# Reordering the last draining slot of an eight-layer attention block ahead of its expert mixture

## The chip, the cores and the metric

The kernel runs on one core of one Trainium2 chip, as one program. The metric is the device time in microseconds of one execution. A core has five engines that run their own instruction streams in order and wait for each other by semaphores: TensorE (PE in the profile, with its weight loads as PEld), VectorE (DVE), ScalarE (ACT), GpSimd (POOL) and SyncE (SP), which only issues transfers here.

## The reference

The input is 8 sequences of 256 rows of 128 features, in float32. A conditioning vector gives a shift, a scale and a gate for two halves. The first half is eight layers of linear attention with a feed-forward of width 512; the second is a mixture of eight routed experts (the best two of each row) and a shared one.

```
h = layernorm(x) * (1 + ca) + sa
for each of 8 layers:
    q, k, v = h Wq + bq, h Wk + bk, h Wv + bv
    Q, K = elu(q) + 1, elu(k) + 1
    V = Q * sum(K * v) / (Q * sum(K) + eps)
    h = layernorm(gelu(V Wo + bo) + h) * ln1_s + ln1_b
    h = layernorm(gelu(gelu(h Wf1 + bf1) Wf2 + bf2) + h) * ln2_s + ln2_b      # FF1, FF2, the last norm
x = x + ga * h
h = layernorm(x) * (1 + cb) + sb
s = softmax(h router_w);  keep the two largest of 8
y = shared(h) + sum over experts of s_e * (silu(h gate_e) * (h up_e)) down_e
out = x + gb * y
```

## The kernel before, in words

The 2048 rows are cut into four chunks (`CH = 4`) of 512 rows; features lie on the 128 partitions. A piece of work (chunk c in layer l) has number n = 4 l + c, from 0 to 31 (`NI = 32`). The layers are software-pipelined in slots. Slot s holds four pieces at different stages: a = s (queries, keys, values), b = s - 1 (the output projection, the first norm), f = s - 2 (FF1 and FF2) and d = s - 3 (the last norm). Each engine has a function `slot` that writes its own share of a slot, and the order of its lines is the order on that engine; no scheduler moves anything. After the 32 full slots come two draining slots. In the first, `slot(NI, 0, ...)`, b, f and d are left. In the second, `slot(NI + 1, 1, ...)`, only f = 31 (chunk 3) and d = 30 (chunk 2) are left; this is the one that the change touches. Extra work is hooked into a slot by name: `run(extra, "place")` calls what the caller has given for that place.

Behind the draining slots comes the mixture. It runs in units: unit i of chunk c is `divmod(i, 10)`; units 0 and 1 of a chunk are halves of the shared expert, units 2 to 9 the routed experts. A unit is a gate product and an up product on TensorE, Silu on ScalarE, a product of the two on VectorE, and a down product on TensorE. Units 0 and 1 of the first chunk are plain float32 (`product`, L509), and a 128x512 float32 product is recorded as two matmuls. From unit 2 on every product is three matmuls of rounded operands (L511 to L513): the high part of weight and input (`wu_hi`, `h_hi`, written by ScalarE), and the low parts (`wu_lo`, `h_lo`, written by GpSimd in `split_weights_lo` L868 and `split_h` L883). `h_hi` and `h_lo` are the tiles xs_hi0, xs_lo0 and so on, so the profile shows them under those names. `ORDER` is the order in which the weights of the units are split. In the same way sg is the tiles ek and eq (the Silu of a unit), and su is mk and mq.

What the second draining slot does on each engine, and what waits for what:

- TensorE (L430 to L446): the last two quarters of FF1 (`ff1(1)`, `ff1(3)`, L404), then at the place "before ff2" the gate and up products of unit 0, then the first quarter of FF2 (L413), the transposes of the normalized piece 30 (xhD, L295, `to_fm["D"]`), the other three quarters of FF2. Behind the slot come the products of unit 1, then `weights_to_fm(0)` (L490), the transposes of the routing weights `cs`, then the gate of unit 2. `up(1)` writes the PSUM bank that FF2 used, so it waits for `g2_ready`. `weights_to_fm(0)` writes the bank that the gate of unit 0 used, so it waits for the first Silu (`sg_ready`). The gate of unit 2 waits for `h_hi`, `h_lo` and the first low part of the weights.
- ScalarE (L698 to L720): four Gelus of FF1, three splits `wu_hi`, the scale and shift of the last norm (`xs`, L712), then the Gelu of FF2 (L783), a table load, and the Silus of units 0 and 1 (L790), `scaled(1)` (zf) and the copy of the routing weights (cst, L759).
- GpSimd: the sum y2 = g2 + x2 of piece 30 (L844), the reciprocal root of the last norm's variance (rsD, L830, a power on 128x4), two weights' low parts, then the sum of piece 31 (L877), `split_h(0)`, two more low parts.
- VectorE: the first half of the routing (`route_scores`: mx, lg, cmp_gt, cmp_eq), the statistics of the last norm (stD, ..., veD, meanD), its normalization (xhD, L945), then `route_compare` (cmp_lo, cmp_all), ranks and weights (`cs`).

Of the kernel before, what the change touches and what calls it, by code (L numbers as in the profile page):

```python
# [30 lines left out]
def adaln_block(nc, x, w_qkv, w_o, w_f1, w_f2, v_a, v_bo, v_ln1, v_bf1, v_bf2, v_ln2, c_t, w_mod,  # L31
                w_router, w_unit, ident_in, select_in, lower_in, out):

    with ExitStack() as ctx:
# [145 lines left out]
        def has(n):  # L180

            return not isinstance(n, int) or 0 <= n < NI
# [107 lines left out]
        def _(pe):  # L290
# [32 lines left out]
            def slot(s, c, l, extra=None):  # L323
# [106 lines left out]
                if has(f):  # L430
                    ff1(1)
                    ff1(3)
                run(extra, "before ff2")
                if has(f):
                    ff2(0)
                run(extra, "middle")
                if has(b):
                    pe.wait_ge(y1_ready, b + 1)
                    transposes(ps_b, y1, to_tm["B"])
                if has(d):  # L440
                    pe.wait_ge(normed["D"], d + 1)
                    transposes(ps_d, xh["D"], to_fm["D"])
                if has(f):
                    ff2(1)
                    ff2(2)
                    ff2(3)  # L446

            slots(pe, slot, {"middle": rest_to_fm})


# [144 lines left out]
            keep_awake(9, ps_q)  # L595
            slot(NI + 1, 1, LAYERS, {"start": scores_0, "before ff2": unit_0})

# [31 lines left out]
        def _(act):  # L629
# [31 lines left out]
            act.wait_ge(consts_set, 4)  # L661

            def slot(s, c, l, extra=None):
                a, b, f, d = s, s - 1, s - 2, s - 3
# [28 lines left out]
                for j in range(FJ):  # L693
# [12 lines left out]
                    if j == 3 and has(a) and splits_next(s, c):  # L706
                        split_qkv_hi(l + 1)
                    if j == 3 and has(d):
                        act.wait_ge(to_fm["D"], d + 1)
                        if (c - 3) % CH == 0:  # L710
                            act.wait_ge(ld["vln2"], 4 * d + 16)
                        nc.scalar.activation(xs[(c - 3) % CH][:], ps_d[:], ACT.Identity,  # L712
                                             bias=vln2[:, 1:2], scale=vln2[:, 0:1]).then_inc(x_ready, 1)
                        if has(s + 1):
                            act.wait_ge(v_mm, d + 1)
                            nc.scalar.activation(xs_hi[(c - 3) % CH][:], ps_d[:], ACT.Identity,
                                                 bias=vln2[:, 1:2], scale=vln2[:, 0:1]).then_inc(x_hi_ready, 1)
# [66 lines left out]
            for i in range(CH * U):  # L784
# [3 lines left out]
                if i >= 2:  # L788
                    act.wait_ge(su_ready, i - 1)
                nc.scalar.activation(sg[i % 2][:], gates(i)[:], ACT.Silu).then_inc(sg_ready, 1)  # L790
                if splits(i) > splits(i - 1):

# [25 lines left out]
        def _(pool):  # L818
# [21 lines left out]
            def slot(s, c, l, extra=None):  # L840
                a, b, d = s, s - 1, s - 3
                if has(d):
                    pool.wait_ge(g2_ready, d + 1)
                    nc.gpsimd.tensor_tensor(y2[:], g2[:], x2[(c - 3) % CH][:], ALU.add).then_inc(y2_ready, 1)  # L844
                    rstd("D", d)
                if has(b):
# [23 lines left out]

            slots(pool, slot, None, None, {"last": lambda: split_x_lo(CH - 1, 0)})
            slot(NI, 0, LAYERS, {"end": lambda: rstd("F", 0)})
            split_weights_lo(ORDER[:2])
            slot(NI + 1, 1, LAYERS)
            split_weights_lo(ORDER[2:4])
            pool.wait_ge(g2_ready, NI)
            nc.gpsimd.tensor_tensor(y2[:], g2[:], x2[CH - 1][:], ALU.add).then_inc(y2_ready, 1)  # L877

            def split_h(c):
# [5 lines left out]

            split_h(0)
            split_weights_lo(ORDER[4:6])
            for i in range(FIRST, CH * U - 2):
# [20 lines left out]
        def _(dve):  # L909
# [230 lines left out]
            slot(NI, 0, LAYERS, {"within the last norm": select_rounded, "after the last norm": residual_0, "within the first norm": lambda: second_norm(0)})  # L1140
            slot(NI + 1, 1, LAYERS, {"before the last norm": lambda: route_scores(0)})
            route_compare(0)
            route_ranks(0)
# [93 lines left out]
```

## Time and profile before

| | us |
|---|---|
| median of 3 runs | 539.97 |
| lowest and highest | 539.44, 540.39 |
| the profiled execution | 542.1 |
| its span, first to last instruction | 540.3 |
| TensorE busy in the span | 507.2 (94%) |
| VectorE, ScalarE, GpSimd busy | 434.7, 407.7, 295.2 |
| mean granted TensorE clock | 0.989 of full speed |
| span of 400 to 420: TensorE busy | 19.85 |
| span of 420 to 440: TensorE busy | 16.90 |
| span of 440 to 460: TensorE busy | 15.92, at a clock of 0.91 |

The layers take the span up to about 410 us, the second draining slot lies at 409 to 420, the mixture behind it. Times are read as microseconds from the span's start. Busy time is that of the engine's records; TensorE's matmuls overlap by their tails, so the distance from one start to the next says what a matmul costs in a row of them, and not its recorded length. In brackets stand the idle time before an instruction and what ended it.

### The profile page before, as it was taken

How to read it: one execution, taken by the hardware profiler on the slowest of the kernel's cores; microseconds unless marked ns; L12 is line 12 of the kernel's file. 1: busy time of each engine (PE TensorE's matmuls, PEld its weight loads, DVE VectorE, ACT ScalarE, POOL GpSimd, SP SyncE). 2: the span in 40 equal slices, each digit the busy share in tenths (PEclk: the TensorE clock that was granted, in tenths of full speed). 3: DMA queues.
4: the chain of work that ended last, by engine and by line, in shares of the span. 5: the costliest groups of instructions: out<-in, count | busy, mean ns of one | idle time of the engine just before them, and what ended most of it. 6: DMA issues, size and time to landing. Idle time of an engine off the chain costs nothing.

```text
span 540.3 us, 8177 instructions
## 1 busy us (share of the span) xinstructions
PE 507.2 (94%) x1958; PEld 307.4 (57%) x1958; DVE 434.7 (80%) x1638; ACT 407.7 (75%) x594; POOL 295.2 (55%) x322
## 2 busy tenths in 40 slices
PE   2879999999999999999999999999999986999996
PEld 2335555565555556555555555555546565777784
DVE  4767988888888888889888888888887575977753
ACT  1748887888888888888888788888887555575752
POOL 3226556655565566555655665556545573555552
PEclk9979999999999999999999999999999998999999
DMA  7200000001000100100010010001000000000000
GB/s 245 82 0 16 6 21 20 15 5 39 15 5 5 34 15 5 39 15 0 5 39 15 5 36 18 0 5 39 0 2 0 1 1 2 0 19 2 20 13 28
DMA packets 15911, 11.22 MB, mean 21 GB/s; under 512 B 8189, under 2 KB 13693, under 8 KB 15893
## 3 DMA queue, kind: packets, MB, share of 16 engines
q1 hardware_dynamic: 15316, 10.42, 6.9%
q10 hardware_dynamic: 576, 0.60, 0.4%
q8 instruction: 7, 0.11, 0.1%
q14 instruction: 12, 0.09, 0.1%
HBM read 9.96 MB, written 1.05 MB: 20 GB/s over the span
## 4 chain that ended last, share of the span: by engine, by line
PE 80%; DVE 11%; issue 3%; POOL 2%; ACT 2%; DMA 1%; SPq 0%; ACTq 0%; DVEq 0%; POOLq 0%
PE bank L413 19%; PE bank L404 14%; PE bank L295 12%; PE bank L427 5%; PE bank L401 5%; PE bank L331 4%; PE bank L336 4%; PE bank L332 4%; PE bank L511 2%; PE bank L513 2%; PE bank L512 2%; PE bank L571 1%; DMA x<-in_x 1%; PE bank L556 1%; PE bank L559 1%
## 5 line engine op out<-in xcount | busy, mean ns | idle before, releaser
L413 PE MATMUL bank<-hid,wf 128*128 128x512 f32 x256 | 120.4, 593 | 0.0
L830 POOL TENSOR_TENSOR rsD<-veD,c_half 128x4 f32<-128x4 f32 x32 | 37.8, 1180 | 104.3 <-DVE veD L931 104.3
L404 PE MATMUL bank<-x,wf 128*128 128x512 f32 x192 | 93.0, 593 | 0.0
L698 ACT ACTIVATE hid<-bank,vbf 128x512 f32<-128x512 f32 x128 | 77.6, 693 | 0.3 <-PE bank L404 0.3
L902 POOL TENSOR_TENSOR xs_lo<-sc,xs_hi 128x512 fp32r<-128x512 f32 x36 | 47.8, 1327 | 46.9 <-ACT xs_hi L798 46.9
L413 PEld LDWEIGHTS bank<-hid,wf 128*128 128x128 f32 x256 | 46.0, 190 | 46.0 <-issue 30.6
L404 PEld LDWEIGHTS bank<-x,wf 128*128 128x128 f32 x192 | 35.1, 190 | 33.2 <-issue 16.2
L985 DVE TENSOR_SCALAR x<-bank,vln 128x256 f32<-128x256 f32 x64 | 31.9, 540 | 26.5 <-PE bank L295 26.5
L945 DVE TENSOR_SCALAR xhB<-bank,meanB,rsB 128x128 f32<-128x128 f32 x128 | 43.7, 405 | 7.8 <-POOL rsB L830 7.8
L945 DVE TENSOR_SCALAR xhD<-bank,meanD,rsD 128x128 f32<-128x128 f32 x128 | 43.7, 405 | 6.9 <-POOL rsD L830 2.7
L848 POOL TENSOR_TENSOR y<-g,xs 128x512 f32<-128x512 f32 x32 | 40.7, 1272 | 13.6 <-ACT g L692 13.5
L669 ACT ACTIVATE g<-bank,vbf 128x512 f32<-128x512 f32 x31 | 21.4, 690 | 34.7 <-PE bank L413 34.7
L295 PEld LDWEIGHTS bank<-ident,y 128*128 128x128 f32 x256 | 29.5, 140 | 31.4 <-POOL y L848 14.7
L331 PE MATMUL bank<-xs_hi,wqkv_hi 128*128 128x512 f32 x87 | 43.5, 500 | 1.4 <-DVE wqkv_lo L1057 0.6
L295 PE MATMUL bank<-ident,y 128*128 128x128 f32 x256 | 39.8, 278 | 4.4 <-ACT cst L759 2.3
L830 POOL TENSOR_TENSOR rsB<-veB,c_half 128x4 f32<-128x4 f32 x32 | 32.8, 1024 | 19.9 <-DVE veB L931 19.9
L672 ACT ACT_TABLE_LOAD x32 | 41.1, 1283 | 0.6
L692 ACT ACT_TABLE_LOAD x32 | 41.1, 1283 | 0.6
L844 POOL TENSOR_TENSOR y<-g,x 128x512 f32<-128x512 f32 x31 | 39.7, 1281 | 1.0 <-ACT g L669 1.0
L838 POOL TENSOR_TENSOR xs_lo<-xs,xs_hi 128x512 fp32r<-128x512 f32 x29 | 38.5, 1326 | 0.0
L427 PE MATMUL bank<-vt,wo 128*128 128x512 f32 x64 | 35.0, 628 | 1.1 <-DVE vt L1001 1.1
L336 PE MATMUL bank<-xs_lo,wqkv_hi 128*128 128x512 f32 x87 | 34.6, 452 | 0.0
(157 smaller groups left out, 1186.9 us busy)
## 6 DMA issues: line engine op xcount, KB each, us to landing
wf<-in_w_f SPq DMA_DIRECT2D x16, 256.0 KB, 2.6
wu<-in_w_unit SPq DMA_DIRECT2D x10, 192.0 KB
wqkv<-in_w_qkv SPq DMA_DIRECT2D x7, 192.0 KB, 2.4
x<-in_x SPq DMA_DIRECT2D x4, 256.0 KB, 6.7
out<-ot SPq DMA_DIRECT2D x4, 256.0 KB, 2.1
wo<-in_w_o SPq DMA_DIRECT2D x8, 64.0 KB, 1.8
wmod<-in_w_mod ACTq DMA_DIRECT2D x1, 384.0 KB, 4.0
vln<-in_v_ln SPq DMA_DIRECT2D x16, 1.0 KB, 1.7
```

The source lines that it names most:

```text
L295: mm = nc.tensor.transpose(out_bank[:, j * P:(j + 1) * P], t, ident[:])
L331: nc.tensor.matmul(bank[:], wqkv_hi[:, w], xs_hi[c][:], start=True, stop=False)
L336: return nc.tensor.matmul(bank[:], wqkv_hi[:, w], xs_lo[c][:], start=False, stop=True)
L404: mm = nc.tensor.matmul(ps_ff[j][:], wf1[:, j * P:(j + 1) * P], x2[(c - 2) % CH][:], start=True, stop=True)
L413: mm = nc.tensor.matmul(ps_f0[:], wf2[:, j, :], hid[:, j, :], start=(j == 0), stop=(j == FJ - 1))
L427: nc.tensor.matmul(ps_b[:], wo[:], vt[(c - 1) % CH][:], start=True, stop=True).then_inc(wo_mm, 1)
L672: nc.scalar.preload_act_table_set(LN_SET)
L692: nc.scalar.activation(g1[:], ps_b[:], ACT.Gelu_apprx_tanh, bias=vbo[:, 0:1]).then_inc(g1_ready, 1)
L698: nc.scalar.activation(hid[:, j, :], ps_ff[j][:], ACT.Gelu_apprx_tanh, bias=vbf1[:, j:j + 1]).then_inc(h_ready, 1)
L830: nc.gpsimd.tensor_tensor(rs[buf(k, n)][:], ve[buf(k, n)][:], c_half[:], ALU.pow).then_inc(rstd_ready[k], 1)
L902: nc.gpsimd.tensor_tensor(sc_lo[k % 2][:], sc[i % 3][:], sc_hi[k % 2][:].bitcast(F32), ALU.subtract).then_inc(sc_lo_ready, 1)
L945: ap = nc.vector.tensor_scalar(rows_of(k, n)[:, j, :], src[:, j, :], mean[q][:, j:j + 1], rs[q][:, j:j + 1], ALU.subtract, ALU.mult)
```

## The change

On TensorE, in the slot without a piece b, the four quarters of FF2 come directly behind FF1, then the transposes of the last norm, then unit 0 and unit 1. On ScalarE the last norm's scale is written behind the first Silu. On GpSimd `split_h(0)` and the low part of the third weight in `ORDER` go between the sum y2 and rsD, three low parts follow rsD, and the sum of piece 31 comes last. On VectorE `route_compare(0)` goes ahead of the last norm's normalization. No instruction is added or removed, and the slots of the layers are written as before.

```diff
-                run(extra, "before ff2")
                 if has(f):
                     ff2(0)
                 run(extra, "middle")
...
-                if has(d):
+
+                def last_norm_to_fm():
                     pe.wait_ge(normed["D"], d + 1)
                     transposes(ps_d, xh["D"], to_fm["D"])
+
+                if has(d) and has(b):
+                    last_norm_to_fm()
                 if has(f):
                     ff2(1)
                     ff2(2)
                     ff2(3)
+                if has(d) and not has(b):
+                    last_norm_to_fm()
+                run(extra, "behind ff2")
...
-            slot(NI + 1, 1, LAYERS, {"start": scores_0, "before ff2": unit_0})
+            slot(NI + 1, 1, LAYERS, {"start": scores_0, "behind ff2": unit_0})
...
-                    if j == 3 and has(d):
+                    if j == 3 and has(d) and has(b):
+                        last_norm(c, d)
...
                 nc.scalar.activation(sg[i % 2][:], gates(i)[:], ACT.Silu).then_inc(sg_ready, 1)
+                if i == 0:
+                    last_norm(1, NI - 2)
...
                     nc.gpsimd.tensor_tensor(y2[:], g2[:], x2[(c - 3) % CH][:], ALU.add).then_inc(y2_ready, 1)
+                    run(extra, "behind the sum")
                     rstd("D", d)
...
+            def first_low_parts():
+                split_h(0)
+                split_weights_lo(ORDER[2:3])
+
             slot(NI, 0, LAYERS, {"end": lambda: rstd("F", 0)})
             split_weights_lo(ORDER[:2])
-            slot(NI + 1, 1, LAYERS)
-            split_weights_lo(ORDER[2:4])
+            slot(NI + 1, 1, LAYERS, {"behind the sum": first_low_parts})
+            split_weights_lo(ORDER[3:6])
             pool.wait_ge(g2_ready, NI)
             nc.gpsimd.tensor_tensor(y2[:], g2[:], x2[CH - 1][:], ALU.add).then_inc(y2_ready, 1)
-            split_h(0)
-            split_weights_lo(ORDER[4:6])
...
-            slot(NI + 1, 1, LAYERS, {"before the last norm": lambda: route_scores(0)})
-            route_compare(0)
+            slot(NI + 1, 1, LAYERS, {"before the last norm": lambda: route_scores(0),
+                                     "within the last norm": lambda: route_compare(0)})
             route_ranks(0)
```

TensorE before, from the second half of FF1 in the second draining slot to the gate of unit 2 (x2_3 is the input of FF1, hid that of FF2, hf0 that of the mixture; bank2 takes the gate of unit 0 and then the routing weights, bank3 the sum of FF2 and then the up product of unit 1):

```order
L404 MATMUL bank4<-x2_3,wf1 128x512
L404 MATMUL bank0<-x2_3,wf1 128x512
L509 MATMUL bank2<-hf0,wu 128x512
L509 MATMUL bank5<-hf0,wu 128x512
L413 MATMUL bank3<-hid,wf2 128x512
L295 MATMUL bank6<-ident,xhD 128x128 x4
L413 MATMUL bank3<-hid,wf2 128x512 x3
L509 MATMUL bank4<-hf0,wu 128x512
L509 MATMUL bank3<-hf0,wu 128x512
L490 MATMUL bank2<-ident,cs 16x128 x4
L511 MATMUL bank0<-xs_hi0,wu_hi 128x512
```

And TensorE now, at the same place:

```order
L404 MATMUL bank4<-x2_3,wf1 128x512
L404 MATMUL bank0<-x2_3,wf1 128x512
L413 MATMUL bank3<-hid,wf2 128x512 x4
L295 MATMUL bank6<-ident,xhD 128x128 x4
L515 MATMUL bank2<-hf0,wu 128x512
L515 MATMUL bank5<-hf0,wu 128x512
L515 MATMUL bank4<-hf0,wu 128x512
L515 MATMUL bank3<-hf0,wu 128x512
L496 MATMUL bank2<-ident,cs 16x128 x4
L517 MATMUL bank0<-xs_hi0,wu_hi 128x512
```

Unit 0 (banks 2 and 5) has moved behind FF2 and the transposes, so that eight recorded matmuls of units 0 and 1 now stand between FF2 and the routing weights, where four stood.

GpSimd before, from the sum of piece 30 to the first low part of a unit's product (xs_lo0 from hf0 is `h_lo`):

```order
L844 TENSOR_TENSOR y2<-g2,x2_2 128x512
L830 TENSOR_TENSOR rsD<-veD,c_half 128x4
L868 TENSOR_TENSOR wu_lo<-wu,wu_hi 128x384 x2
L877 TENSOR_TENSOR y2<-g2,x2_3 128x512
L883 TENSOR_TENSOR xs_lo0<-hf0,xs_hi0 128x512
L868 TENSOR_TENSOR wu_lo<-wu,wu_hi 128x384 x2
L902 TENSOR_TENSOR xs_lo2<-sc2,xs_hi2 128x512
```

And GpSimd now:

```order
L855 TENSOR_TENSOR y2<-g2,x2_2 128x512
L888 TENSOR_TENSOR xs_lo0<-hf0,xs_hi0 128x512
L880 TENSOR_TENSOR wu_lo<-wu,wu_hi 128x384
L841 TENSOR_TENSOR rsD<-veD,c_half 128x4
L880 TENSOR_TENSOR wu_lo<-wu,wu_hi 128x384 x3
L900 TENSOR_TENSOR y2<-g2,x2_3 128x512
L915 TENSOR_TENSOR xs_lo2<-sc2,xs_hi2 128x512
```

`h_lo` and one weight have moved ahead of rsD, and the sum that waits for the Gelu of FF2 has moved to the end.

## Rows read from the trace of the kernel before

**Rows 1.** The page, part 4: the chain that ended last, by engine.

```profile
PE 80%; DVE 11%; issue 3%; POOL 2%; ACT 2%; DMA 1%; SPq 0%; ACTq 0%; DVEq 0%; POOLq 0%
```

**Rows 2.** Timeline of PE, 412 to 424: start, length, instruction, idle before.

```profile
413.82 1.88 PE L509 MATMUL bank<-hf,wu 128*128 128x512 f32 x4
415.54 1.02 PE L413 MATMUL bank<-hid,wf 128*128 128x512 f32 x2
416.56 0.66 PE L295 MATMUL bank<-ident,xhD 128*128 128x128 f32 x4
417.06 2.74 PE L413 MATMUL bank<-hid,wf 128*128 128x512 f32 x6
419.63 2.07 PE L509 MATMUL bank<-hf,wu 128*128 128x512 f32 x4
422.57 0.60 PE L490 MATMUL bank<-ident,cs 128*16 128x128 f32 x4 [0.88 <-ACT ek L790]
423.44 0.47 PE L511 MATMUL bank<-xs_hi,wu_hi 128*128 128x512 f32 x1 [0.27 <-issue]
```

**Rows 3.** Timeline of ACT, 412 to 425.

```profile
413.17 1.84 ACT L698 ACTIVATE hid<-bank,vbf 128x512 f32<-128x512 f32 x3 [0.29 <-PE bank L404]
...
417.26 0.78 ACT L712 ACTIVATE xs<-bank,vln 128x512 f32<-128x512 f32 x1 [1.01 <-PE bank L295]
419.83 0.69 ACT L783 ACTIVATE g<-bank,vbf 128x512 f32<-128x512 f32 x1 [1.80 <-PE bank L413]
...
421.83 0.60 ACT L790 ACTIVATE ek<-bank 128x512 f32<-128x512 f32 x1
...
424.42 0.60 ACT L790 ACTIVATE ek<-bank 128x512 f32<-128x512 f32 x1 [0.25 <-PE bank L513]
```

**Rows 4.** Timeline of POOL, 404 to 450.

```profile
408.89 1.27 POOL L844 TENSOR_TENSOR y<-g,x 128x512 f32<-128x512 f32 x1
414.01 1.02 POOL L830 TENSOR_TENSOR rsD<-veD,c_half 128x4 f32<-128x4 f32 x1 [3.86 <-DVE veD L931]
415.00 1.96 POOL L868 TENSOR_TENSOR wu_lo<-wu,wu_hi 128x384 fp32r<-128x384 f32 x2
...
421.82 1.27 POOL L883 TENSOR_TENSOR xs_lo<-hf,xs_hi 128x512 fp32r<-128x512 f32 x1
```

**Rows 5.** Timeline of DVE, 404 to 460, around the last norm of piece 30.

```profile
410.57 0.42 DVE L1097 TENSOR_TENSOR cmp_gt<-lg 128x256 f32<-128x256 f32 x1
...
412.37 0.89 DVE L914 BATCH_NORM_STATS2 stD<-bank 128x6 f32<-128x128 f32 x4 [1.03 <-PE bank L295]
...
415.14 1.37 DVE L945 TENSOR_SCALAR xhD<-bank,meanD,rsD 128x128 f32<-128x128 f32 x4 [1.13 <-POOL rsD L830]
...
419.15 0.19 DVE L1122 TENSOR_TENSOR cs<-comb,cs 128x32 fp32r<-128x32 f32 x1
```

**Rows 6.** Timeline of all engines, 443 to 447, rows of DVE and POOL.

```profile
443.27 1.30 POOL L883 TENSOR_TENSOR xs_lo<-hf,xs_hi 128x512 fp32r<-128x512 f32 x1
...
443.63 1.23 DVE L1097 TENSOR_TENSOR cmp_gt<-lg 128x256 f32<-128x256 f32 x1
...
444.52 1.50 POOL L902 TENSOR_TENSOR xs_lo<-sc,xs_hi 128x512 fp32r<-128x512 f32 x1
...
444.77 1.52 DVE L1098 TENSOR_TENSOR cmp_eq<-lg 128x256 f32<-128x256 f32 x1
```

**Rows 7.** Timeline of all engines, 243.5 to 245.5, one slot of the layers.

```profile
243.87 1.18 POOL L830 TENSOR_TENSOR rsD<-veD,c_half 128x4 f32<-128x4 f32 x1 [3.43 <-DVE veD L931]
...
244.59 0.42 DVE L1024 TENSOR_SCALAR mq<-eq 128x512 f32<-128x512 f32 x1
```

**Rows 8.** Timeline of PE, 430 to 460.

```profile
448.73 0.50 PE L571 MATMUL bank<-cst,sel 128*128 128x512 f32 x1 [1.81 <-DVE sc L1177]
...
457.68 0.63 PE L295 MATMUL bank<-ident,y 128*128 128x128 f32 x4 [2.28 <-ACT cst L759]
```

**Rows 9.** Windows: length, busy of PE, PEld, DVE, ACT, POOL, then PEclk.

```profile
449.00:453.00 4.00, 4.00 (x12) 3.13 (x12) 2.99 (x9) 1.56 (x3) 2.58 (x2) 0.57 0.01 2
```

More of the change, by code:

```diff
@@ L661, in _, with last_norm @@
             act.wait_ge(consts_set, 4)
+            def last_norm(c, d):
+                act.wait_ge(to_fm["D"], d + 1)
+                if (c - 3) % CH == 0:
+                    act.wait_ge(ld["vln2"], 4 * d + 16)
+                nc.scalar.activation(xs[(c - 3) % CH][:], ps_d[:], ACT.Identity,
+                                     bias=vln2[:, 1:2], scale=vln2[:, 0:1]).then_inc(x_ready, 1)
             def slot(s, c, l, extra=None):
@@ L707, in slot @@
                         split_qkv_hi(l + 1)
-                    if j == 3 and has(d):
[L709 to L713, printed above, removed]
+                    if j == 3 and has(d) and has(b):
+                        last_norm(c, d)
                         if has(s + 1):
@@ L871, in _ @@
             slots(pool, slot, None, None, {"last": lambda: split_x_lo(CH - 1, 0)})
-            slot(NI, 0, LAYERS, {"end": lambda: rstd("F", 0)})
-            split_weights_lo(ORDER[:2])
-            slot(NI + 1, 1, LAYERS)
-            split_weights_lo(ORDER[2:4])
-            pool.wait_ge(g2_ready, NI)
-            nc.gpsimd.tensor_tensor(y2[:], g2[:], x2[CH - 1][:], ALU.add).then_inc(y2_ready, 1)
             def split_h(c):
@@ L884, in split_h @@
                                         ALU.subtract).then_inc(h_lo_ready, 1)
-            split_h(0)
-            split_weights_lo(ORDER[4:6])
+            def first_low_parts():
+                split_h(0)
+                split_weights_lo(ORDER[2:3])
+            slot(NI, 0, LAYERS, {"end": lambda: rstd("F", 0)})
+            split_weights_lo(ORDER[:2])
+            slot(NI + 1, 1, LAYERS, {"behind the sum": first_low_parts})
+            split_weights_lo(ORDER[3:6])
+            pool.wait_ge(g2_ready, NI)
+            nc.gpsimd.tensor_tensor(y2[:], g2[:], x2[CH - 1][:], ALU.add).then_inc(y2_ready, 1)
             for i in range(FIRST, CH * U - 2):
```

## The prediction

> **What bounds the kernel now.** I read the page first. Its chain that ended last is 80% TensorE [rows 1], so only a change of what TensorE waits for can move the end. I then took TensorE's timeline through the stretch that the diff touches, the second draining slot and the start of the mixture, and last the timelines of ScalarE, GpSimd and VectorE there, to see who releases each wait.
>
> The reader is to see in [rows 2] that TensorE is dense up to the end of unit 1 and then stops twice. Matmuls of 128x512 in float32 start 0.43 us apart (four from 413.82 to 415.54). The two of FF2's first quarter should give way at 416.40, and the transposes of xhD start at 416.56, when VectorE has ended xhD at 415.14 + 1.37 = 416.51 [rows 5]. The four transposes take 0.50 from their start to the next row's. The last four matmuls of the draining part (unit 1) take 2.07 and not 1.88: `up(1)` waits for the Gelu of FF2, which ends at 419.83 + 0.69 = 420.52 [rows 3]. Then L490 starts at 422.57 on the first Silu (421.83 to 422.43), though unit 1 had ended its starts at 419.63 + 1.72 + 0.19 = 421.54: 1.03 lost, of which the profile calls 0.88 idle. Last, the gate of unit 2 starts at 423.44. From L490's start to that it is 0.87. Four transposes took 0.50 above with the change to the next kind of row in it; these write 16 rows in place of 128, and I take 0.40 for them, so 0.47 are lost, of which 0.27 is marked idle. That is put down to "issue", but GpSimd ends `h_lo` at 421.82 + 1.27 = 423.09 [rows 4], so that is the wait.
>
> **The change part by part.** It adds and removes nothing, so the sum is the idle time that goes. From 413.82 to 423.44 TensorE has to do: FF2, eight matmuls at 0.43 = 3.44; four transposes 0.50; units 0 and 1, eight matmuls = 3.44; L490, 0.40. That is 7.78 in 9.62 us, 1.84 less. The four losses above (0.16, 0.19, 1.03, 0.47) make 1.85, the same within rounding. It comes in full if nothing is late in the new order. I take the waits one by one.
>
> FF2 starts at 413.82 in place of 415.54. Its quarters need the four hidden Gelus; three of them run from 413.17 and end at 415.01 [rows 3], and the last quarter is reached at 413.82 + 2.58 = 416.40. Nothing waits. FF2 ends its starts at 417.26.
>
> The transposes of xhD are then reached at 417.26, where xhD was ready at 416.51, so there is 0.75 of room. Two edits eat into it. GpSimd now does `h_lo` (1.27) and one weight (0.98, half of the 1.96 for two in rows 4) between the sum, which ends at 410.16, and rsD, which starts at 414.01: both are over before rsD can start, so rsD itself is not held. `h_hi`, which `h_lo` needs, is written by ScalarE before that sum ends. But they now lie beside cmp_gt and cmp_eq on VectorE, and [rows 6] show what that does: cmp_gt takes 1.23 and not the 0.42 of [rows 5], and ends 0.29 behind the end of GpSimd's subtraction (444.57); cmp_eq again takes 1.52 and ends 0.27 behind the next (446.02), which itself takes 1.50 and not 1.30. Laid on the new order: `h_lo` ends at 411.43, cmp_gt at 411.72, the weight's low part at 411.43 + 0.98 + 0.20 = 412.61, cmp_eq at 412.88. The statistics stD started at 412.37, when the transposes of y2 were done; now they start at about 412.92, 0.55 late. This carries to rsD (414.56) and to the start of the normalization (415.69). The other edit, cmp_lo and cmp_all ahead of the normalization, costs 2 x 0.42 and two gaps of 0.05, 0.94, and fits in the 1.13 for which VectorE waits for rsD [rows 5]. xhD is then ready at 417.06 + 0.05. TensorE comes at 417.26: still not late. If the port costs nothing, the room is 0.75; if cmp_lo and cmp_all are held too, it turns into a stall (first rival). So the price of these two edits is 0 to 1.25, and I take 0, the end that the nearest row speaks for: [rows 7] show VectorE's mq, 0.42 for 128x512, fully inside a power of GpSimd on 128x4 (243.87 to 245.05): the power does not hold VectorE off.
>
> The Trainium skill, page "SBUF — State Buffer", section "SBUF: two separate sides", says that the shared port pair is an exclusive lock for the whole instruction and that the other engine fully blocks, for a VectorE operation in a two-port mode or with two SBUF inputs. Rows 6 agree. Rows 7 do not where GpSimd's instruction is the power; what the rule would make of this change is the first rival.
>
> Unit 0 follows at 417.26 + 0.50 = 417.76, unit 1 at 419.48, and L490 is reached at 421.20. `up(1)` starts at 420.34 and needs the Gelu of FF2. That Gelu started 0.19 behind the last start-to-start of FF2 (417.06 + 2.58 = 419.64, to 419.83), so now 417.45, and ends at 418.14: the 0.19 are gone. ScalarE is free for it, since the scale of the last norm no longer stands ahead. The first Silu came 2.00 behind the Gelu's start (421.83 - 419.83, the table load in it), so now at 419.45, and ends at 420.05: 1.15 before L490 asks for it. The scale (0.78, rows 3) goes behind it and pushes the second Silu to about 420.6, when its gate (419.48 + 0.86 = 420.34) is done. It also pushes what follows. From the first Silu to that of unit 2 it was 424.42 - 421.83 = 2.59, 0.25 of it idle; with the scale in it, 2.34 + 0.78 = 3.12, so ScalarE is free for the Silu of unit 2 at 422.57. TensorE will have its gate done at 424.42 - 1.84 = 422.58. This is a tie; a tenth late would be hidden, since TensorE still has the up products of unit 2, a down product and a broadcast ahead of what needs it. That broadcast needs the moved scale (ended by 420.9) and the routing weights' copy, which precedes the Silu of unit 2, and stands two microseconds behind the gate.
>
> The routing weights `cs` were done at 419.34, 2.83 behind the end of xhD [rows 5], with cmp_lo and cmp_all in it (0.94 at least). So seven small operations take 1.9 at most, and now start at 417.1 behind xhD. But three low parts and the sum of piece 31 (from about 415.6 to 419.8 on GpSimd) lie beside them. With none held, `cs` comes at 419.0; with three of them held by 0.8 each, as cmp_gt was, at 421.4, 0.2 behind the moment when L490 is reached. So 0 to 0.2, taken as 0.
>
> Every low part is earlier than it was: `h_lo` at 411.4, the first three weights by 412.6, the next three by about 418.8. The sum of piece 31 ends by 419.9 and is first read at 457.68 [rows 8]. So the gate of unit 2 starts at 421.20 + 0.40 = 421.60 against 423.44. Behind it every engine waits for what TensorE started there, and no transfer is in play, so the mixture moves as one piece.
>
> Sum: -1.84 + 0 + 0 = -1.84. The profiled execution took 542.1 (span 540.3, 1.8 around it) and would take 540.3. The median of the runs is 539.97, 2.1 below the profiled one; the stretch is short and has no transfers in it, so I take the same difference from the median: 538.1.
>
> **The rivals.**
>
> *The port held for every instruction.* If the power did hold VectorE off, cmp_lo (issued at 414.6) would wait for the end of rsD at 415.58 and end at 415.87; the next low part would end at 415.6 + 1.2 = 416.8 and cmp_all at 417.1; xhD at 418.5. TensorE stands from 417.26 to 418.5, 1.25. `cs` is then done about 420 to 422, at the time when L490 comes. Net -0.6: 539.4. For it: rows 6. Against: rows 7. The page of the Trainium skill named above, taken at its word, would give this time.
>
> *The clock, once more.* Right behind an idle time of 1.81 [rows 8] TensorE's granted clock falls: from 449 to 453 it is 0.57 of full speed [rows 9], which means that for most of this stretch it stood at the lower of its two levels, 1.2 GHz. Against full speed that costs 4.00 x (1 - 0.57) = 1.72. Behind the longer idle time of 2.28 [rows 8] the profile shows no such stretch. So length alone does not decide, and a mixture that runs 1.8 earlier may meet it elsewhere. One stretch more: -1.84 + 1.72 = -0.1, 539.9. One less: -3.6, 536.4.
>
> *Slower: the clock, twice more.* The same mechanism, with its place in the mixture's idle times (before 448.73, before 457.68, and later ones). It decides from 1.84 us of added half-speed time, more than one stretch: two cost 3.44, net +1.6, 541.6. For it: the mixture keeps its idle times, and one was followed by the lower level. Against: the longer one was not, and the change takes idle time away ahead of them.
>
> *It does not do what it says.* If the wait for `h_lo` or the first Silu only changed hands, for instance if the Silu is held by the table load, L490 would move less. That load began when the Gelu had ended, since the Silu came 1.31 behind it, and nothing else stands before it, so I see no place for this and fold its chance into the first rival.
>
> **How the numbers follow.** Forecast 0.72; the port 0.09, 539.4; one more half-speed stretch 0.07, 539.9; one less 0.06, 536.4; two more 0.06, 541.6. What a measurement can tell from no change is 0.2%, 1.08 us: below 538.9 is faster, above 541.0 slower. Faster: 0.72 + 0.06 = 0.78. Same: 0.09 + 0.07 = 0.16. Slower: 0.06. The forecast's own range is 537.6 to 538.7 (the price of the port from 0 to 0.7, and the scatter of the runs shown). The range runs from the case of one less, 536.4, to a little over the port's, 539.6; it leaves out the two higher cases, 0.13 together.
>
> **What would show it.** In the profile after: FF2's eight matmuls at once behind FF1, xhD's transposes without idle time in front, units 0 and 1 in one row of eight, L496 (the former L490) directly behind with no wait for ScalarE, and the gate of unit 2 at about 421.6. cmp_gt and cmp_eq of the first chunk longer together by some 1.5 us. The first Silu at about 419.5 and the scale behind it. The prediction is wrong if the transposes of xhD wait for VectorE by more than 0.3, if L496 waits for `cs`, or if the distance from the gate of unit 2 to the end of the span (540.3 - 423.4 = 116.9) is not what it was within a few tenths; a longer one with a clock of 0.50 in a further window is the clock's doing.

## The result and the profile after

| | before | changed |
|---|---|---|
| median, us | 539.82 (13 runs) | 535.88 (13 runs) |
| lowest, highest | 537.56, 541.40 | 534.94, 538.27 |
| the profiled execution, its span | 542.1, 540.3 | 535.88, 533.7 |
| mean granted TensorE clock in it | 0.989 | 1.00 |

The ratio is 0.9928, with a 95% interval of 0.9909 to 0.9947: faster by 3.9 us, twice the 1.84 that were forecast, and outside the range. (One later run of the kernel before, of 737.73 us, was in a slow state and is left out of everything below.) The draining slot did what was forecast. TensorE's timeline of the changed kernel, 408 to 419 (columns as in [rows 2]):

```profile
409.00 1.88 PE L404 MATMUL bank<-x,wf 128*128 128x512 f32 x4
410.72 3.60 PE L413 MATMUL bank<-hid,wf 128*128 128x512 f32 x8
414.15 0.64 PE L295 MATMUL bank<-ident,xhD 128*128 128x128 f32 x4
414.62 3.60 PE L515 MATMUL bank<-hf,wu 128*128 128x512 f32 x8
418.06 0.60 PE L496 MATMUL bank<-ident,cs 128*16 128x128 f32 x4
418.42 0.48 PE L517 MATMUL bank<-xs_hi,wu_hi 128*128 128x512 f32 x1
```

No row has idle time. From the second half of FF1 (L404 x4) to the gate of unit 2 it is 418.42 - 409.00 = 9.42. Before it was 423.44 [rows 2] - 412.10 = 11.34, from this row of the kernel before:

```profile
412.10 1.88 PE L404 MATMUL bank<-x,wf 128*128 128x512 f32 x4
```

So 1.92 are won (forecast 1.84). I call this distance the draining distance below. The other engines there, first VectorE:

```profile
407.47 1.09 DVE L1110 TENSOR_TENSOR cmp_gt<-lg 128x256 f32<-128x256 f32 x1
408.48 1.22 DVE L1111 TENSOR_TENSOR cmp_eq<-lg 128x256 f32<-128x256 f32 x1
409.73 0.89 DVE L927 BATCH_NORM_STATS2 stD<-bank 128x6 f32<-128x128 f32 x4
...
411.28 0.42 DVE L1115 TENSOR_TENSOR cmp_lo<-cmp_eq,lower 128x256 f32<-128x256 f32 x1
411.73 0.43 DVE L1116 TENSOR_TENSOR cmp_all<-cmp_gt,cmp_lo 128x256 f32<-128x256 f32 x1
412.71 1.37 DVE L958 TENSOR_SCALAR xhD<-bank,meanD,rsD 128x128 f32<-128x128 f32 x4 [0.55 <-POOL rsD L841]
```

then GpSimd:

```profile
407.01 1.26 POOL L888 TENSOR_TENSOR xs_lo<-hf,xs_hi 128x512 fp32r<-128x512 f32 x1
408.23 1.18 POOL L880 TENSOR_TENSOR wu_lo<-wu,wu_hi 128x384 fp32r<-128x384 f32 x1
411.37 1.21 POOL L841 TENSOR_TENSOR rsD<-veD,c_half 128x4 f32<-128x4 f32 x1 [1.95 <-DVE veD L944]
```

and ScalarE:

```profile
414.35 0.69 ACT L792 ACTIVATE g<-bank,vbf 128x512 f32<-128x512 f32 x1 [1.21 <-PE bank L413]
...
416.35 0.60 ACT L799 ACTIVATE ek<-bank 128x512 f32<-128x512 f32 x1
416.85 0.77 ACT L673 ACTIVATE xs<-bank,vln 128x512 f32<-128x512 f32 x1
```

cmp_gt and cmp_eq are held by GpSimd (2.31 together, against twice the 0.42 of [rows 5]). cmp_lo starts 0.09 before the power rsD, and cmp_all lies wholly inside it (411.73 to 412.16, the power from 411.37 to 412.58); they take their usual 0.42 and 0.43, and the power 1.21 in place of the 1.02 of [rows 4]. xhD ends at 414.08, and TensorE comes for it at 410.72 + 3.44 = 414.16: 0.08 in hand. The first Silu ends at 416.95, 1.11 before the L496 that waits for it. The routing weights `cs` are written at 417.17, 0.89 before it.

Where are the other 4.7 us of the 6.6 by which the two profiled spans differ? Windows of the kernel before (columns as in [rows 9]):

```profile
25.00:40.00 15.00, 10.52 (x25) 4.75 (x26) 9.83 (x39) 7.47 (x9) 3.34 (x5) 0.77 0.00 0
445.00:455.00 10.00, 8.19 (x31) 6.17 (x30) 7.49 (x16) 5.71 (x9) 3.79 (x4) 0.83 0.00 1
```

and of the changed kernel, the second moved with the mixture:

```profile
25.00:40.00 15.00, 10.47 (x35) 5.11 (x34) 9.61 (x37) 9.50 (x14) 5.70 (x9) 1.00 0.00 0
440.00:450.00 10.00, 7.02 (x32) 4.97 (x30) 7.48 (x16) 6.82 (x13) 4.87 (x4) 1.00 0.00 1
```

The reader is to see the PEclk of 0.77 and 0.83 against 1.00: the kernel before has stretches in which TensorE runs at half of its full clock, which I call half-speed stretches, and this profile of the changed kernel has none in these windows. The L404 row already starts 3.1 earlier (409.00 against 412.10), from the start of the program, which the change doesn't touch. From the gate of unit 2 to the end of the span it is 533.7 - 418.42 = 115.28 against 116.86: 1.58 less, with the same instructions. So 6.6 = 3.1 + 1.9 + 1.6, and only the middle term is the new order's own. The question of the experiments was whether the rest is luck of the two profiled executions or belongs to the change.

### The profile page after: what moved, and what is told of

It is laid out like the page before. It is cut to its first block, busy times and chain, and to the rows that moved or that the text cites. A ratio compares the mean times of both kernels' runs of the same rounds, so it can differ in the third digit from the quotient of the medians.

```text
span 533.7 us, 8177 instructions
## 1 busy us (share of the span) xinstructions
PE 501.3 (94%) x1958; PEld 304.6 (57%) x1958; DVE 437.0 (82%) x1638; ACT 407.7 (76%) x594; POOL 295.7 (55%) x322
## 3 DMA queue, kind: packets, MB, share of 16 engines
HBM read 9.96 MB, written 1.05 MB: 21 GB/s over the span
## 4 chain that ended last, share of the span: by engine, by line
PE 81%; DVE 11%; issue 3%; POOL 2%; ACT 2%; DMA 1%; SPq 0%; ACTq 0%; DVEq 0%; POOLq 0%
PE bank L413 19%; PE bank L404 14%; PE bank L295 12%; PE bank L427 5%; PE bank L401 5%; PE bank L331 4%; PE bank L336 4%; PE bank L332 4%; PE bank L519 2%; PE bank L517 2%; PE bank L518 2%; PE bank L577 1%; PE bank L562 1%; DMA x<-in_x 1%; DVE sc L1190 1%
## 5 line engine op out<-in xcount | busy, mean ns | idle before, releaser
L404 PE MATMUL bank<-x,wf 128*128 128x512 f32 x192 | 93.0, 593 | 0.0
L404 PEld LDWEIGHTS bank<-x,wf 128*128 128x128 f32 x192 | 35.0, 189 | 33.3 <-issue 16.3
L860 POOL TENSOR_TENSOR y<-g,xs 128x512 f32<-128x512 f32 x32 | 40.8, 1275 | 11.5 <-ACT g L705 11.3
```

The lines of the kernel that those rows point to most:

```text
L404: mm = nc.tensor.matmul(ps_ff[j][:], wf1[:, j * P:(j + 1) * P], x2[(c - 2) % CH][:], start=True, stop=True)
```

## The experiments

The runs fall into four groups (e1 to e4, e5 to e8, e9 to e12, e13 to e16), each with its own runs of the kernel before beside it; their medians were 540.22, 540.78, 539.80 and 540.58, their mean clocks 0.9910, 0.9889, 0.9904 and 0.9895. The ratios are taken within a group; medians and clocks of different groups compare less well. "Clock" is the mean over a kernel's runs of the granted clock; "draining" and "to the end" are the draining distance and the distance from the gate of unit 2 to the end of the span, in its profile.

| kernel | median us | ratio [95%] | clock | draining | to the end |
|---|---|---|---|---|---|
| before, repeated (e1) | 541.00 | 1.0001 [0.9982, 1.0020] | 0.9898 | 11.34 | 116.80 |
| changed, repeated (e2) | 537.08 | 0.9942 [0.9920, 0.9964] | 0.9928 | 9.43 | 115.35 |
| TensorE's order alone (e3) | 537.98 | 0.9977 [0.9952, 1.0003] | 0.9911 | 10.07 | 116.88 |
| the rest alone (e4) | 540.10 | 1.0005 [0.9986, 1.0024] | 0.9906 | 11.51 | 116.85 |
| before, mixture filled (e5) | 538.49 | 0.9963 [0.9937, 0.9989] | 0.9938 | 11.34 | 115.29 |
| changed, mixture filled (e6) | 537.16 | 0.9935 [0.9912, 0.9958] | 0.9930 | 9.43 | 115.27 |
| changed, moved back 17 (e7) | 539.26 | 0.9983 [0.9962, 1.0005] | 0.9900 | 11.27 | 116.79 |
| before, drain filled (e8) | 541.73 | 1.0012 [0.9982, 1.0042] | 0.9883 | 11.35 | 117.39 |
| before, pushed 18 (e9) | 540.94 | 1.0036 [1.0009, 1.0063] | 0.9900 | 12.78 | 115.23 |
| changed, GpSimd as before (e10) | 537.17 | 0.9946 [0.9925, 0.9968] | 0.9935 | 9.38 | 115.29 |
| before, start filled (e11) | 538.13 | 0.9962 [0.9945, 0.9979] | 0.9968 | 11.34 | 116.80 |
| changed, start filled (e12) | 536.38 | 0.9944 [0.9922, 0.9965] | 0.9972 | 9.43 | 115.28 |
| before, both filled (e13) | 537.25 | 0.9938 [0.9918, 0.9958] | 0.9996 | 11.34 | 115.22 |
| changed, both filled (e14) | 534.93 | 0.9894 [0.9867, 0.9921] | 0.9990 | 9.41 | 115.24 |
| changed, moved back 5 (e15) | 538.84 | 0.9967 [0.9946, 0.9989] | 0.9917 | 9.96 | 115.93 |
| changed, moved back 11 (e16) | 539.53 | 0.9980 [0.9955, 1.0005] | 0.9900 | 10.61 | 115.25 |

**The two kernels again.** e1 is the kernel before and e2 the changed one, without an edit.

> The kernel before, word for word, as a second program: what the comparison gives for no change, and a second profile of it. Theory A (the 1.84 us of the draining slot are shifted in full, and the rest of the measured 3.9 is TensorE's clock, which falls to its lower level by chance of the execution): ratio 1.000 within 0.3%; the distance from the second half of FF1 in the second draining slot (L404 x4) to the gate of unit 2 is 11.3 us again; the profile's half-speed stretches (span 28 to 37 and 449 to 453 before) lie elsewhere or are absent, and the runs' spans go down as their clock goes up. Theory B (the stretch at 449 to 453 belongs to the order of the kernel before, by the idle time in its draining slot): it is there again, between the broadcast that waits for sc and the routing weights' transposes of chunk 1.

> The changed kernel again, with a second profile. Both theories: ratio 0.990 to 0.996 to the kernel before; the distance from the second half of FF1 (L404 x4) to the gate of unit 2 is 9.4 us again, 1.9 less. Theory A: with the clock at full in both, the spans differ by 1.9; some of these runs have a half-speed stretch in the mixture too. Theory B: no run of this kernel has one in the mixture.

Both draining distances repeat to 0.01. e1 has the half-speed stretch behind the same broadcast, e2 has none there. Theory A had called that chance. Against the runs beside it e2 gains 3.1 us (0.9942), less than the 3.9 of the first comparison, though inside its interval. Over all groups the kernel before gave 130 runs with a recorded clock and the changed one 19 (13 of them from the first comparison), which can be laid side by side by their clock:

| clock of the run | before: runs, mean us | changed: runs, mean us |
|---|---|---|
| under 0.9875 | 34, 541.8 | 0 |
| 0.9875 to 0.9905 | 42, 540.7 | 3, 538.1 |
| 0.9905 to 0.9935 | 40, 539.4 | 2, 537.6 |
| 0.9935 to 0.9965 | 6, 538.4 | 8, 536.0 |
| over 0.9965 | 8, 538.3 | 6, 535.7 |

In a row the kernels differ by 1.8 to 2.6. The rest is that the changed kernel's runs stand in lower rows of the table. 3 and 2 runs in two of the rows are few. That the changed kernel has the better clock rests most on the first comparison: its 13 runs have a mean of 0.9954, e2's six have 0.9928, only 0.0018 above the kernel before beside them, and e10's twelve (the changed kernel but for GpSimd, below) 0.9935, 0.0031 above.

**The parts.** e3 takes TensorE's half of the diff, e4 everything else.

```diff
# e3, on the kernel before; e4 is the changed kernel with the same lines turned back
-                run(extra, "before ff2")
...
+                if has(d) and not has(b):
+                    last_norm_to_fm()
+                run(extra, "behind ff2")
```

> Only TensorE's order is changed (FF2, last norm's transposes, then units 0 and 1); ScalarE, GpSimd and VectorE are as in the kernel before. From the rows of before: the scale of the last norm stands ahead of the Gelu of FF2 again and waits for the transposes (reached at 417.26 in the time of before, so it runs 417.9 to 418.6), so the Gelu ends at 419.3, the first Silu at 421.2 (L490 asks at 421.2), the sum of piece 31 at 420.6 and h_lo at 421.8; gate of unit 2 at 422.1 against 421.6 in the full change and 423.4 before. So the distance from FF1's second half to it is 10.0 (before 11.3, full change 9.4). If instead the other engines' moves are what counts: 11.3. Ratio 0.996 to 0.998 with equal clocks.

> Only ScalarE, GpSimd and VectorE are changed, TensorE's order is that of before. h_lo is early, so the 0.47 before the gate of unit 2 go; cmp_gt and cmp_eq are held by GpSimd (together 2.3 and not 0.84), so xhD comes 0.3 to 0.55 later, and here TensorE asks for it at 416.40 with no room, so FF2 and with it the Gelu and the first Silu are late by that. Distance from FF1's second half to the gate of unit 2: 11.2 to 11.5, no gain. If low parts were the bound in the draining slot: 10.9 or less.

Both distances came as expected: 10.07 (10.0) and 11.51 (11.2 to 11.5). In e3 ScalarE's timeline shows why 0.65 are missing:

```profile
414.35 0.78 ACT L718 ACTIVATE xs<-bank,vln 128x512 f32<-128x512 f32 x1 [1.65 <-PE bank L295]
415.02 0.68 ACT L789 ACTIVATE g<-bank,vbf 128x512 f32<-128x512 f32 x1
```

The Gelu of FF2 stands behind the scale, and `h_lo` behind the sum behind the Gelu. In e4, xhD is late by the port and TensorE waits for it (timeline of PE):

```profile
414.07 0.65 PE L295 MATMUL bank<-ident,xhD 128*128 128x128 f32 x4 [0.68 <-DVE xhD L952]
```

**GpSimd's move by itself.** e10 is the changed kernel with `split_h(0)` and the low parts where they were.

```diff
-            slot(NI + 1, 1, LAYERS, {"behind the sum": first_low_parts})
-            split_weights_lo(ORDER[3:6])
+            slot(NI + 1, 1, LAYERS)
+            split_weights_lo(ORDER[2:4])
             (the sum of piece 31)
+            split_h(0)
+            split_weights_lo(ORDER[4:6])
```

> The changed kernel with GpSimd's order of before (h_lo behind the sum of piece 31). In e3 the gate of unit 2 came 0.65 later than in the full change; there the Gelu of FF2 stood behind the scale of the last norm. With ScalarE's move kept, the Gelu ends at 415.04 (times of the changed kernel's profile), the sum at 416.35, h_lo at 417.6, and the gate is reached at 418.42: distance from FF1's second half 9.4, the same as the full change. cmp_gt and cmp_eq take 0.42 each again. If GpSimd's move carries a gain of its own, the distance is 9.9 (0.47 more). Time within 0.2% of the changed kernel by either, if the clock is the same.

9.38: the move of the low parts is worth nothing once the Gelu comes early. e10 keeps ScalarE's and VectorE's moves, which e3 lacks; of the two it is ScalarE's one instruction that e3's timeline points at. No run moved it alone.

**Filling the mixture's idle time.** Transposes of the identity into banks that nobody reads at that time:

```diff
+                    if u == 6 and n == 1: pe.wait_ge(x_new, 2);    keep_awake(14, ps_q)   # ahead of norm_to_fm
+                if i == 9:                pe.wait_ge(hf_ready, 2); keep_awake(16, ps_v)   # ahead of the broadcast
+                if i == U + 2:            pe.wait_ge(lg_ready, 2); keep_awake(18, ps_q)   # ahead of last_to_tm
```

> The kernel before, with transposes of the identity into free PSUM banks placed on TensorE where the mixture of the first two chunks waits: 14 ahead of the transposes of xhF, 16 ahead of the broadcast that waits 1.81 for sc, 18 ahead of the transposes that wait 2.28 for cst. They start about 0.11 us apart, so they fill 1.5, 1.8 and 2.0 us of idle time and delay nothing by more than 0.1. Both theories: the half-speed stretch that the profiles of the kernel before, of its repeat and of both half changes have behind that broadcast (3.3 to 3.4 us, worth 1.7) is gone, the mean clock of the runs goes up from 0.991 by 0.003 to 0.994, the median down by 1 to 1.7: ratio 0.997 to 0.998. If filling does not hold the clock: ratio 1.000 to 1.001.

> The changed kernel with the same fillers. Theory A2 (the change raised the clock only by where its idle times fall, and it is still at risk of a half-speed stretch in the mixture): median 0.3 to 1 us lower than the changed kernel. Both: with fillers in both, the two kernels differ by the draining slot alone, 1.9 (e5 to e6: 0.9965). If the change had its extra 2 us from anywhere but the clock, e5 and e6 would still be 3.5 to 4 apart.

e5's window (8.19 and 0.83 in the kernel before):

```profile
445.00:455.00 10.00, 9.94 (x56) 8.09 (x55) 8.29 (x17) 6.80 (x11) 5.37 (x5) 1.00 0.01 2
```

The fillers hold the clock, and the kernel before gains 0.37% by them (2.0 us) without any change of its own work. The changed kernel gains nothing (537.16 against 537.08 and 535.88): it had no stretch there to lose in its profiles. The medians of e5 and e6 are 1.3 apart, their means 1.7, where the kernels themselves were 3.9 apart. With the mixture's waits filled in both, nothing is left beyond the 1.92 of the draining slot, within the scatter of 12 runs each.

**Position or idle time?** e7 gives the gain back as dense work ahead of the mixture, e8 takes the draining slot's idle time away and leaves the mixture where it was. In these cuts and the next two the `wait_ge` ahead of the transposes is left out.

```diff
 # e7, on the changed kernel, behind weights_to_fm(0)     # e8, on before
+  if i == 2: keep_awake(17, ps_q)                        +  if i == 1: keep_awake(8, ps_q)   # ahead of weights_to_fm(0)
                                                          +  if i == 2: keep_awake(3, ps_q)
```

> The changed kernel, with 17 transposes of the identity between the routing weights' transposes and the gate of unit 2: the 1.9 us won in the draining slot are given back as dense work of TensorE, with no idle time, so the mixture stands where it stood before. Theory P (the half-speed stretch depends on where the mixture's idle times fall in time, counted from the start of the program): it is back in the profile behind the broadcast that waits for sc, mean clock 0.991, ratio 0.999 to 1.001. Theory I (it depends on the idle time in the draining slot, which is gone here too): no such stretch, mean clock 0.995, ratio 0.996 to 0.997.

> The kernel before, with 8 transposes ahead of the routing weights' transposes and 3 ahead of the gate of unit 2, into idle time only: the draining slot has no idle time to speak of and the mixture starts within 0.1 of where it did. Theory P: nothing changes, stretch in the profile, mean clock 0.991, ratio 0.999 to 1.001. Theory I: no stretch, mean clock 0.995, ratio 0.996 to 0.997.

e7's mean clock is 0.9900, where e2 has 0.9928 and the first runs of the changed kernel 0.9954. Its ratio alone would not show that: the 1.84 us put back are 0.0034, and 0.9942 + 0.0034 = 0.9976 lies inside e7's interval. Its windows have the PEclk of the kernel before to the digit:

```profile
25.00:40.00 15.00, 10.88 (x27) 5.24 (x28) 8.71 (x32) 7.40 (x10) 4.30 (x6) 0.77 0.00 0
445.00:455.00 10.00, 6.75 (x24) 4.96 (x23) 5.77 (x14) 5.30 (x11) 3.88 (x3) 0.83 0.00 1
```

and e8, with no idle time in its draining slot, has two stretches in the mixture:

```profile
445.00:455.00 10.00, 7.95 (x29) 5.73 (x27) 6.86 (x16) 5.20 (x9) 3.81 (x4) 0.83 0.00 1
455.00:465.00 10.00, 8.00 (x32) 6.58 (x33) 5.87 (x18) 4.09 (x9) 3.76 (x4) 0.83 0.01 2
```

So theory I is out: e8 has no better clock than the kernel before beside it (0.9883 against 0.9889), and e7 has the stretch without idle time in the draining slot. Theory P is left, that what counts is when the mixture's idle times come. Three more positions:

```diff
+  if i == 2: keep_awake(18, ps_q)      # e9, on before;  5 and 11 on the changed kernel: e15, e16
```

> The kernel before, with 18 transposes of the identity between the routing weights' transposes and the gate of unit 2. The gate starts 1.5 us later, with dense work ahead of it. Theory P (where the mixture's idle times fall, counted from the start of the program, decides on the half-speed stretch): 1.9 us earlier lost it, and 1.5 us later may lose it too; then the mean clock goes from 0.990 to 0.993 or more and the added 1.5 cost little: ratio 0.998 to 1.001. Theory N (the stretch has nothing to do with the position, e7 and e8 showed it by chance): clock 0.990, ratio 1.003.

> The changed kernel with 5 transposes (0.55 us) ahead of the gate of unit 2, so the mixture starts 0.5 later, dense. If the position decides smoothly, between none (mean clock 0.994) and 17 (0.990): 0.993, and 0.5 to 0.9 us over the changed kernel. If there is an edge in it, 0.994 and +0.5, or 0.990 and +1.9.

> The same with 11 transposes (1.2 us). Smooth: clock 0.9915, 2.0 us over the changed kernel. If position plays no part and e7 was chance: clock 0.994, +1.2.

On the changed kernel the mean clock is lower with more transposes, 0, 5, 11 and 17: 0.9946 (19 runs), 0.9917, 0.9900, 0.9900. But these stand in different groups. Against the kernel before in the same group it is +0.0018 (e2), +0.0023, +0.0005 and +0.0011, each known to 0.002 or 0.003 only, so the steps between them are not shown. By the ratios e15 stands 1.4 us above e2 and 2.1 above the first comparison, 0.5 of it its own dense work, and the intervals overlap. e9, on the far side, is a partial miss: its profile has no stretch in the mixture, and 3 of its 12 runs have a clock of 0.995 or more, but 5 have 0.984. Theory P had hoped for more; the ratio is what theory N said. The runs of one kernel scatter over both cases; that position shifts the shares is likely and not proved.

The profiles tell more than theory P. Counted from the start of the span, position does not decide: the gate of unit 2 starts at 420.45 in both e2 and e4, and only e4 has the stretch. Counted from the end of the start's own stretch it fits, in the three profiles where that end is the same, 36.01 in e1 and e15 and 36.02 in e2. Windows of e1, then of e15, with the mixture's waits from their timelines of PE:

```profile
29.18:36.01 6.83, 5.79 (x10) 2.06 (x8) 3.70 (x18) 2.60 (x4) 1.27 (x2) 0.50 0.00 0
36.01:449.01 413.00, 404.48 (x1540) 233.40 (x1539) 352.03 (x1406) 341.97 (x484) 239.07 (x264) 1.00 0.06 14
449.01:452.43 3.42, 3.42 (x10) 2.64 (x9) 2.68 (x8) 1.23 (x2) 2.38 (x2) 0.50 0.01 2
...
448.37 0.50 PE L571 MATMUL bank<-cst,sel 128*128 128x512 f32 x1 [1.81 <-DVE sc L1177]
```

```profile
29.18:36.01 6.83, 5.74 (x10) 2.06 (x8) 3.67 (x18) 2.64 (x4) 1.23 (x2) 0.50 0.00 0
36.01:455.85 419.84, 410.15 (x1572) 238.44 (x1572) 359.01 (x1417) 346.56 (x494) 243.11 (x267) 1.00 0.05 14
455.85:459.26 3.41, 3.41 (x12) 2.73 (x10) 2.03 (x8) 1.09 (x2) 2.24 (x2) 0.50 0.03 5
...
447.05 0.50 PE L577 MATMUL bank<-cst,sel 128*128 128x512 f32 x1 [1.81 <-DVE sc L1193]
454.46 0.63 PE L295 MATMUL bank<-ident,y 128*128 128x128 f32 x4 [2.28 <-ACT cst L771]
```

The same wait of 1.81 is followed by the lower clock in e1, where it ends at 448.37, and not in e15, where it ends 1.32 earlier; there the wait of 2.28 is. In e2 it ends at 445.73 and neither is. In before, e1, e7 and e8 the clock falls 413.0 behind the end of the start's stretch (before: 449.42 - 36.41), but 0.17 to 1.03 behind the end of the wait; in e4, the fifth profile with both, whose stretch at the start is half as long, it falls 416.4 behind. So the time of the fall goes with the start's stretch, and not with the end of the wait.

**The start.** Slots 1 and 2 filled in the same way (e11, e12), and both places filled (e13, e14).

```diff
+  slot 1: keep_awake(6, ps_y) ahead of v, 8 ahead of the output projection, 18 ahead of the transposes of y1
+  slot 2: keep_awake(14, ps_y) ahead of v
```

> The kernel before, with fillers in slots 1 and 2 (6, 8 and 18 transposes in slot 1, 14 in slot 2, into the bank of the modulation) where TensorE waits 0.7 to 2.1 us between 20 and 31 us of the span. Half-speed stretches between 25 and 40, which come in most profiles, of 3 to 12 us, should go: mean clock 0.996, runs closer together, median 1.5 to 2.5 us lower (ratio 0.996); the stretch behind the broadcast in the mixture stays, as theory P has it while the mixture moves no further than the spread of the runs. If the fillers do not hold the clock at the start, ratio 1.000 to 1.002.

> The changed kernel with the same fillers at the start. With the start at full clock in both, e11 and e12 differ by the draining slot (1.9) and by the mixture's half-speed stretch (1.7, if e11 has it and e12 has not): 3.6. If the stretch comes in both or in none, 1.9. This should be the fastest kernel so far: 533.5 to 535, ratio 0.988 to 0.991.

> The kernel before with the fillers of e5 (mixture) and of e11 (start) together. No half-speed stretch at either place: mean clock 0.998 or more in most runs, 536.5 to 537.5, ratio 0.993 to 0.995.

> The changed kernel with both sets of fillers. With the clock at full in both, e13 and e14 differ by the draining slot alone: 1.9 (1.6 to 2.2). If they differ by 3 or more, the extra of the measured 3.9 is not the clock. 534.5 to 535.5, ratio 0.989 to 0.992, the fastest median of all kernels.

The start's stretches go. e11 still has one in the mixture in its profile and e12 has none, but over the runs their clocks are equal (0.9968, 0.9972), and they differ by 1.75, not by the 3.6 that I expected. Three of e12's six runs have a clock of 0.995 to 0.996, as the profiles with one stretch in the mixture alone have (0.995 in e11, 0.996 in e3), so the changed kernel probably meets the stretch in some of its executions too. With the start at full clock the changed kernel has no better clock than the kernel before. e13 and e14, at 0.9996 and 0.9990, differ by 2.3 in median and in mean (1.9 expected, 1.6 to 2.2 allowed for, so 0.1 over that, and well under the 3 that would have spoken against the clock); in their profiles the draining distances differ by 1.93 and the ways to the end by 0.02. e14's windows:

```profile
25.00:40.00 15.00, 13.74 (x65) 8.27 (x63) 10.49 (x39) 9.46 (x13) 4.70 (x7) 1.00 0.01 1
440.00:455.00 15.00, 14.62 (x86) 12.03 (x85) 10.59 (x27) 9.82 (x17) 6.20 (x6) 1.00 0.01 2
```

It is the fastest median of all, 534.93, 1.1% under the kernel before, with 5 runs.

## Why the prediction was wrong

**The order on TensorE: right.** 1.92 against 1.84, with FF2, transposes and units in one dense row. The price of the port was right too: the statistics start 0.73 behind the second half of FF1 and not 0.27, 0.46 late (0.55 forecast), xhD 0.08 ahead of TensorE (0.15 forecast), the power no hindrance to cmp_lo and cmp_all, as [rows 7] had it. The Silu came 7.35 behind the second half of FF1, as worked out (419.45 - 412.10). `cs` came 8.17 behind it, between the two cases worked out (6.9 and 9.3). By the Trainium skill, page "SBUF — State Buffer", section "SBUF: two separate sides", cmp_all with its two SBUF inputs should have waited for the power, which had started before it; it took 0.43 inside it, so the measurement decides against the rule for this GpSimd instruction, and for it with the subtractions.

**GpSimd's move: its own gain was counted in a loss that two edits remove.** The 0.47 of wait for `h_lo` go by the early Gelu alone (e10). The sum was not harmed.

**The step that failed** is "the stretch is short and has no transfers in it, so I take the same difference from the median", with the chance of 0.06 given to one half-speed stretch less. It takes the clock's losses outside the draining slot as the same before and after. They were not, and the prediction's own sign of being wrong came: from the gate of unit 2 to the end it is 115.28 and not 116.9. The stretch behind the broadcast was in the profiles of the kernel before, e1, e4, e7, e8 and e11, all with the mixture at its old place behind FF1, and in that of e3, 1.3 earlier; it was in none of the changed kernel, e2, e10 and e12, 1.9 earlier. The other positions do not make a smooth row: e9 (1.4 later), e15 (1.4 earlier) and e16 (0.7 earlier) lack it too. Without a stretch the mixture takes 115.2 to 115.4, with this one 116.8 to 116.9, so it costs 1.55 (1.72 forecast). Behind the later wait of 2.28, where e8 and e15 have one, it costs only 0.6 to 0.7 (117.39 against 116.8, 115.93 against 115.25). 1.92 + 1.55 = 3.5 of the 3.9. The case was among the rivals, at 536.4, and its size was nearly right; its chance was argued from two idle times of one profile, as if a single execution showed what the runs do.

**How much of it is luck.** The first comparison is the most favourable of three. e2 gains 3.1 us and e10, with the same draining distance, 2.9. The forecast's ratio, 538.1 / 539.97 = 0.9965, lies just above e2's interval and inside e10's. So the clock's share is 2.0 us in the first comparison and 1.0 to 1.2 in the two others.

**What stays open.** Why the position counts. It seems to count only while the start has its own half-speed stretches (e7 against e11 and e12), and the fall stands 413.0 behind their end in four of five profiles. Whether these stretches set the times of the later falls, or only show times that are set by something else, no run tested. The Trainium skill, page "TensorE: Matmul & The Clock Gate", section "Part 1: The HAM clock gate (the "warmup" mystery)", says that the gate's window is free-running and does not start anew with a kernel. If programs also started evenly over it, and nothing at the start shifted the rest, all positions would be equal over many runs. e7, none of whose 12 runs has a clock over 0.993 where 14 of the changed kernel's 19 do, speaks against the three taken together; which of them fails is not shown. Also open are 0.4 us, between the 2.3 of e13 and e14 and the 1.92 of the trace, within the scatter of 9 and 5 runs.

## What to carry to other kernels

Before a difference of profiled spans is explained, split it at two or three instructions that both traces have: here 6.6 fell into 3.1 of start, 1.9 of the change and 1.6 of clock. Where an idle time of TensorE is followed by a stretch at its lower clock, an edit ahead of it that moves it in time can put that stretch at stake, for good or ill, and a forecast needs the clocks of several runs and not of one. The same holds for the measurement: three comparisons of the reordering (the last without GpSimd's move) gave 3.9, 3.1 and 2.9 us. Filling such waits with transposes of the identity into a free bank cost nothing that could be measured here (the draining distances of e8 and e13 are those of the kernel before, to 0.01); at both places it took 3.3 us off the kernel before (540.58 to 537.25), and it makes two kernels comparable.

## What the runs showed of the hardware

- A wait of 1.81 us on TensorE was followed by half-speed clock in one execution (e1) and not in another (e15) whose half-speed stretch at the start was alike to 0.01 us and where the wait ended 1.32 us earlier. In four profiles (before, e1, e7, e8) of the five that have both, the fall came 413.0 us behind the end of the start's half-speed stretch, in the fifth (e4) 416.4.
- A half-speed stretch of 3.4 us cost 1.55 us behind the wait for the broadcast and 0.6 to 0.7 us behind the wait of 2.28 us.
- A power on 128x4 on GpSimd and a two-input VectorE instruction on SBUF run beside each other: 1.21 in place of 1.02 for the one, 0.43 for the other (cmp_all), where its usual time is 0.42. A subtraction on GpSimd, of 128x512 or 128x384, holds the same kind of instruction: cmp_gt and cmp_eq took 1.09 and 1.22 in place of 0.42 and ended 0.29 behind it. In e10, without the subtractions beside them, they took 0.42.
- The clock falls after the wait, not in it: in e7 the wait of 1.83 ends at 446.91, the four products from 447.25 on start 0.23 apart, and only then do they start 0.42 to 0.43 apart.

```profile
446.91 0.51 PE L577 MATMUL bank<-cst,sel 128*128 128x512 f32 x1 [1.83 <-DVE sc L1193]
447.25 0.39 PE L517 MATMUL bank<-xs_hi,wu_hi 128*128 128x512 f32 x1
447.48 0.39 PE L518 MATMUL bank<-xs_hi,wu_lo 128*128 128x512 f32 x1
447.71 0.42 PE L519 MATMUL bank<-xs_lo,wu_hi 128*128 128x512 f32 x1
447.94 0.62 PE L517 MATMUL bank<-xs_hi,wu_hi 128*128 128x512 f32 x1
448.36 0.63 PE L518 MATMUL bank<-xs_hi,wu_lo 128*128 128x512 f32 x1
448.79 0.63 PE L519 MATMUL bank<-xs_lo,wu_hi 128*128 128x512 f32 x1
```
